# Graph layer with attention and experts: the edge sums copied to the row layout inside SBUF

## The reference

```python
xn = layernorm(x)
# graph attention: 4 heads of 64
h = einsum('nd,hdf->nhf', xn, W)
ex = exp(leaky_relu(a_src[src] + a_dst[dst]) - emax[dst])
gnn = segment_sum(h[src] * ex, dst) / segment_sum(ex, dst) + bias
x = x + gnn + linear_attention(xn)
# mixture of experts: 8 experts, 2 for each node
y = layernorm(x) * gamma + beta
logits = y @ Wr + br
w = softmax(top_2(logits))
x = x + sum over the 2 chosen e of w[e] * (gelu(y @ W1[e] + b1[e]) @ W2[e] + b2[e])
```

## Time and profile before

| what | value |
|---|---|
| time, median of 3 runs | 2964.16 us (2961.24 to 2968.06) |
| the profiled execution, own time | 2967.08 us |
| its span in the profile | 2965.3 us |
| mean granted TensorE clock | 0.624 of full |
| main stage and what follows it | to about 2237 us |
| rows stage | about 2237 to 2501 us |
| experts' stage | about 2510 us to the end |

### The profile page before, as it was taken

The page is one execution under the profiler, slowest core; times in us unless marked ns, Lnnn a source line. Parts: engine busy times, 40 slices in busy tenths (PEclk is TensorE's granted clock), DMA queues, the critical chain, the costliest instruction groups (busy, mean ns, idle before and its releaser), DMA issues. The chain is left out here.

```text
span 2965.3 us, 59475 instructions
## 1 busy us (share of the span) xinstructions
PE 1602.5 (54%) x17399; PEld 1226.3 (41%) x17399; DVE 1592.4 (54%) x5472; ACT 598.3 (20%) x2020; POOL 1879.0 (63%) x1848
## 2 busy tenths in 40 slices
PE   3666665566665444444444444444440442999995
PEld 2444444444443323232332332332330331888884
DVE  5577766667776556555555555555552762333331
ACT  3522221122221111111111111111111451222221
POOL 1276667777777777777777777777770464344442
PEclk9867776655555555555555555555555555999998
DMA  5255555645554333333334433333339984788886
GB/s 164 88 139 150 147 148 171 179 112 149 148 154 130 107 107 104 105 107 107 107 107 108 107 107 107 107 108 106 107 107 159 216 228 127 201 215 216 214 213 180
DMA packets 276721, 419.61 MB, mean 142 GB/s; under 512 B 69312, under 2 KB 207044, under 8 KB 276344
## 3 DMA queue, kind: packets, MB, share of 16 engines
q0 software_dynamic: 98592, 245.59, 32.8%
q1 hardware_dynamic: 169296, 170.02, 20.1%
q10 hardware_dynamic: 8712, 2.53, 0.5%
HBM read 344.03 MB, written 80.35 MB: 143 GB/s over the span
## 5 line engine op out<-in xcount | busy, mean ns | idle before, releaser
L453 POOL DMA_INDIRECT region<-node_table,region x1612 | 1578.4, 979 | 637.5 <-issue 461.5
L663 PE MATMUL ps_p<-region 128*32 128x65 f32 x12896 | 423.2, 306 | 842.3 <-DVE region L893 841.7
L663 PEld LDWEIGHTS ps_p<-region 128*32 128x32 f32 x12896 | 329.2, 161 | 954.3 <-DVE region L893 623.6
L540 ACT ACTIVATE region<-region 128x16 f32<-128x16 f32 x403 | 86.9, 216 | 1481.7 <-DVE region L887 1477.2
L1650 POOL DMA_INDIRECT sum_rows<-region,rows_of x112 | 174.7, 1559 | 270.7 <-DVE region L1749 246.1
L893 DVE TENSOR_TENSOR region<-region 128x512 f32<-128x512 f32 x403 | 280.3, 696 | 96.6 <-DVE region L877 95.4
L645 PE MATMUL ps_s<-ident,region 128*128 128x128 f32 x403 | 180.9, 449 | 191.9 <-DVE region L887 185.5
L901 DVE SCALAR_TENSOR_TENSOR acc<-ps_p,region,acc 128x65 f32 x806 | 203.5, 284 | 105.2 <-issue 92.7
L873 DVE TENSOR_SCALAR region<-drep,region 128x8 f32 x403 | 102.1, 253 | 287.5 <-issue 286.7
L649 PEld LDWEIGHTS ps_s<-region 128*128 128x128 f32 x806 | 208.2, 304 | 79.7 <-issue 63.6
L649 PE MATMUL ps_s<-region 128*128 128x32 f32 x806 | 228.2, 376 | 0.3 <-ACT region L534 0.3
(11 more groups left out here) (271 smaller groups left out, 2081.6 us busy)
## 6 DMA issues: line engine op xcount, KB each, us to landing
region<-in_W_dram SPq DMA_DIRECT2D x112, 512.0 KB, 4.6
region<-node_table,region POOLq DMA_INDIRECT x1612
xe<-expert_in SPq DMA_DIRECT2D x56, 258.0 KB, 4.0
acc<-base_rows SPq DMA_DIRECT2D x14, 896.0 KB, 11.9
qkv_rows<-region SPq DMA_DIRECT2D x49, 194.0 KB, 2.3
node_table<-region SPq DMA_DIRECT2D x49, 132.0 KB, 1.7
acc<-qkv_rows SPq DMA_DIRECT2D x7, 910.0 KB, 6.4
agg_rows<-acc SPq DMA_DIRECT2D x28, 227.5 KB, 12.9
```

The source lines that it names most:

```text
L453: pool.indirect_dma_start(out=rows[:, s, j, :], out_offset=None, in_=table[:, :], in_offset=bass.IndirectOffsetOnAxis(ap=idx[:, s * SUB + ...
L663: m = pe.matmul(ps_p[s % 2][h * WIN:(h + 1) * WIN, 0:HC], wts[:, s % 2, j, h, :], rows[:, s, j, h * HC:(h + 1) * HC], start=j == 0, stop=j ...
```

## The change

The DRAM tensor `agg_rows` and `to_rows` go. `load` copies the edge sums of its group straight from `acc` into `a_in`: 16 transfers from SBUF to SBUF, one for each head h and each quarter c of the 128 partitions, each of 32 partitions with 7 runs of 65 floats. They stand between the load of `h_in` and that of `x1`, behind the waits of `load`. VectorE waits for 18 transfers where it waited for 3.

```diff
-    agg_rows = nc.dram_tensor("agg_rows", [N_PAD, G_HEADS * HC], F32)
...
-        agg_out = [sem(f"agg_out{i}") for i in range(2)]
...
-            def to_rows(gr):
-                for h in range(G_HEADS):
-                    sp.dma_start(agg_rows[at(gr, GT * P), h * HC:(h + 1) * HC].rearrange("(c w) f -> w c f", w=WIN),
-                                 acc3[h * WIN:(h + 1) * WIN, at(gr, GT * SUB), :]).then_inc(agg_out[gr % 2], 16)
-
             def load(gr, s):
-                sp.wait_ge(agg_out[s], slot_count(gr, s, 64, 2))
                 if not isinstance(gr, int) or gr >= 2:
                     sp.wait_ge(x1_ready, gr - 1)
                     sp.wait_ge(x1_out, gr * 16 - 16)
                     sp.wait_ge(n_ready, gr * GT - GT)
                 sp.dma_start(h_in[:, s], table[at(gr, GT * P), 0:AW].rearrange("(t p) c -> p t c", p=P)).then_inc(row_in[s], 16)
-                sp.dma_start(a_in[:, s], rows_of(agg_rows, gr)).then_inc(row_in[s], 16)
+                for h in range(G_HEADS):
+                    runs = acc3[h * WIN:(h + 1) * WIN, at(gr, GT * SUB), :].rearrange("p (t c) f -> p t c f", c=SUB)
+                    for c in range(SUB):
+                        sp.dma_start(a_in[c * WIN:(c + 1) * WIN, s, :, h * HC:(h + 1) * HC],
+                                     runs[:, :, c, :]).then_inc(row_in[s], 16)
                 sp.dma_start(x1[:, s], rows_of(base_rows, gr)).then_inc(row_in[s], 16)
...
-            to_rows(0)
-            to_rows(1)
             for gr in range(2):
                 load(gr, gr)
-                to_rows(gr + 2)
             for gr in range(GROUPS):
                 store(gr, gr % 2)
                 if gr + 2 < GROUPS:
                     load(gr + 2, gr % 2)
-                if gr + 4 < GROUPS:
-                    to_rows(gr + 4)
...
-                dve.wait_ge(row_in[s], slot_count(gr, s, 48, 2))
+                dve.wait_ge(row_in[s], slot_count(gr, s, 16 * (2 + G_HEADS * SUB), 2))
```

More of the change, by code:

```diff
@@ L1197, in rows_stage @@
     acc, ident, ones, valid, w_self, region = (g[k] for k in ("acc", "ident", "ones", "valid", "w_self", "region"))
-    table, base_rows, sum_rows, expert_in, agg_rows = (g[k] for k in ("table", "base_rows", "sum_rows", "expert_in", "agg_rows"))
+    table, base_rows, sum_rows, expert_in = (g[k] for k in ("table", "base_rows", "sum_rows", "expert_in"))
     acc3 = acc[:, 0:ACC_C * HC].rearrange("p (c f) -> p c f", f=HC)
```

## The result

| | before | after |
|---|---|---|
| median of the runs | 2965.43 us (4 runs, 2961.24 to 2968.06) | 2945.57 us (4 runs, 2942.79 to 2946.31) |
| span of the profiled execution | 2965.3 us | 2944.3 us |

The ratio is 0.9933 (95% interval 0.9915 to 0.9950): 20 us faster, where 35 were forecast (2929 us). The direction and the place were right, the size was not. The first step is to see where the 15 us are missing.

The account below looks back on a forecast made before the run. GpSimd's sends bound the rows stage, started late by SyncE's transfers. Start 29 us plus middle 6 us is 35 us off 2967.1, 2932 us, or 2929 us as median; range 2918 to 2950 us.

Parts of the forecast that it names:

- What bounds the stage: Rows stage: GpSimd's sends end it; to win are their start, held by SyncE's transfers, and the wait ending four groups.
- X is set by the issue, the packets into SBUF are cheap: Sixteen copies of a group in load take X = 8.2 us, 0.51 us per issue; their packets need half of that.
- The start: Up to GpSimd's first send: attended(0) about 20 us earlier, attended(1) at 2272, first send at 2294.8, 29 us earlier.
- The middle: GpSimd's periods after the first send: 26 us each instead of 27.5, four periods at 1.5 us less, 6 us gained.
- the queue is shorter by 12 us of packets: Reason for 26 us periods in the middle: 12 us less packets in each, though copies and loads still run beside sends.
- From group 4 on nothing changes: End of the rows stage: no gain or loss from group 4 on, nor in the experts' stage, which only starts earlier.
- The store holds nothing: Middle: the store goes out 18.4 us after scales and lands by 26 us; the next load waits until 35 us.
- signs of failure: Forecast falls if copy issues exceed a microsecond, middle x1 waits grow beyond 5 us, or first send comes after 2305.
- Only the start: Rival, 20%: the middle stays at 27.5 us per period, only the start's 29 us are gained; 2935 us.
- Packets as in DRAM: Rival, 15%: packets cost in SBUF what they cost in DRAM, X = 11.2 us; start 20 us earlier, 2944 us.
- A fixed cost of each copy, one after the other: Rival, 7%: each of 16 copies costs p us in sequence; at 1.7 us the kernel is 33 us slower, 2997 us.
- 72 p - 89: Fixed-cost rival's formula for the change in us, p being us per copy; it decides at p = 1.23 us.

Follow-up runs that it names:

- the kernel with early sums: Changed kernel with h_in and the sixteen copies issued before the waits for store and norm, only x1 behind them; 2933.7 us, 31.4 below before.

## Why the prediction was right, and where its size was wrong

*What bounds the stage* was right: GpSimd's chain of sends, begun by `route(0)`, which two loads held back. The last length stayed at 44.3 to 45.4 us in every kernel that leaves GpSimd's sends and waits as they are.

*X is set by the issue, the packets into SBUF are cheap.* Right in kind, shown by the copies cut in two. A packet took 22 ns against 17.8 in the nearest row. The rule of the Trainium skill (DMA: Bandwidth & Descriptors, section Bandwidth) that copies inside SBUF are spared the penalty of short packets agrees with the 22 ns beside the 56 ns of a write into DRAM; the 17.8 ns of a read from DRAM show no penalty either. The term itself was sized too small: 10.4 to 11.5 us for sixteen, and 14.9 in the first load, not 8.2. I had priced an issue by the padding rows and taken the queue behind them as free.

*The start*: forecast 29 us. From the first issue of the padding rows, `attended(0)` came at 23.4 us instead of 19.8, `attended(1)` at 37.2 instead of 33.3, the first send at 60.0 instead of 56.1. 25 us were gained. Of the 3.9 us that are missing, 3.6 are there at `attended(0)`: its `x1` was issued 17.8 us behind that first issue, where the sum had 10.3. VectorE's 13.7 us between the two and the 22.8 us to the send were as in the sum.

*The middle*: forecast 6 us gained, 2.3 us lost, 8.3 us off. The term for the four periods, 26 us each, held: they took 26.3 us each and gained 4.7 us. That is in part luck. I had taken the middle between 24.3 and 27.5 because "the queue is shorter by 12 us of packets", the single periods lie between 22.7 and 28.7 us, and GpSimd's idle time ahead of groups 1 to 4 fell by only 1 us in the mean, from 6.2 to 5.2. The step that failed is "From group 4 on nothing changes": the fifth period took 28.9 us instead of 21.9, 7.0 of the 8.3 us. Its chain starts with load 6. `norm(4)` waited for its slot, so the load went out 13.1 us after `scales(4)` (2378.14 to 2391.23), not 9.2; it ended VectorE's wait 18.2 us later (2409.47), not 15.7; `route(5)`, which stands behind `attended(6)` there, then held GpSimd for 7.0 us. Where VectorE waits for no load, in the kernel with early sums, the fifth period is 23.4 us; with the loads of groups 2 to 6 through DRAM it is 23.4 as well. About 3 us of the 7.0 lie in the sends of group 4 themselves (21.9 us for 19.0). They now run beside the last load and stores, which before were nearly over by then; that this is why is argued, not shown. "The store holds nothing" was right for the changed kernel and became wrong where the issues are doubled.

Of the signs of failure one came near: VectorE's longest wait for `x1` in the middle is 6.1 us, beyond the "present 5 us"; but the kernel before has one of 6.0 us too, ahead of group 5, that the prediction did not list.

*The rivals.* "Only the start", with 20%, is right for the middle as a whole, but not in its mechanism: the period did not stay at 27.5 us, four became shorter and the fifth longer. "Packets as in DRAM" gave nearly the right time (2944 us) by a mechanism that the 22 ns and the cut copies exclude; the 9.7 us beside the copies in its sum are worked out nowhere, and the fixed-cost rival has 6.9 us in the same place. "A fixed cost of each copy, one after the other" was the right mechanism with the wrong point: two issues for a copy, 1.28 us, are 26 us slower than before, where 72 p - 89 gives 3. The slope holds (46 us for 0.63 us more, 73 us for each us), though in the middle by SyncE's chain and not by VectorE's. So the constant of 89 us was too large by some 22 us (at 0.65 us for a copy the formula gives 42 us gained, and 19.9 were), and the point at which the change is worth nothing is an estimated 0.92 us for a copy (0.65 + 19.9 / 73), not 1.23. The rule of the Trainium skill on transfers under 64 KB (the same page, Rules for kernel authors) points the right way, in the issue. The about 2 us that the prediction puts beside it is the page's fixed cost of one transfer issued by GpSimd (section Anatomy of one DMA — SWDGE (gpsimd) path). The runs show 0.65 us for each of SyncE's copies one behind the other; that they overlap shows in the kernel with early sums, where a copy's data lands 4.6 us after its issue in the median.

## What to carry to other kernels

Price a transfer that is cut into many by the issue on its engine, from the same kind of transfer if the trace has one, and ask what stands behind the last of them in that queue: here the largest transfer and the store did. Look at the last period of a pipeline by itself: it may be short because a queue has run empty, and a change that moves work into that queue takes this away. A queue that has less to carry is not by that much a shorter wait; look at which large transfer is issued just before the landing that someone waits for (here a pattern of a few groups, not a proof). Put the large one first and the small copies behind it, and put work that needs no freed buffer ahead of the wait for that buffer.

## What the runs showed of the hardware that I had not expected

An issue of a copy inside SBUF of 32 partitions takes 0.59 to 0.61 us, and one of 16 partitions, with half the packets, the same: the source line of the kernel with the copies cut in two has

```profile
L1281 SPq DMA_DIRECT2D acc<-acc x224: 585/599/3132, 2245.4 to 2449.1; - x112
```

The first issue of a load, with nothing just ahead of it, takes 0.36 us, though it carries four times the packets of a copy. The landing of GpSimd's last sends of group 0 took 6.2 us in the changed kernel, with `x1` and a store, 1.8 MB, issued 1.5 and 0.9 us ahead of their end, and 2.1 us with `x1` first, where the store went out 1.6 us behind it. The sixteen copies of a load were issued in 10.4 us at best in the changed kernel, and in up to 18.1 us in the kernel with early sums.
